# Layer-2 matrices: another order of loads and splits, with part of the split on GpSimd

## What is computed

```python
x = x + L0(x): x @ W0.T + bias0 + scale[id0] * (x @ A0[id0].T) @ B0[id0].T
x = x + L1(x): x @ W1.T + bias1 + (x @ A1[id1].T) @ B1[id1].T
x = x + L2(x): einsum('bsi,boi->bso', x, weight2[id2])      # 8 matrices of 1024 x 1024
x = x + L3(x): einsum('bct,bcd->bdt', x, weight3[id3])      # 64 x 64, over the rows
```

## Time and profile before

| what | us |
|---|---|
| median of 3 runs | 625.91 |
| the runs | 622.2, 625.91, 628.33 |
| the profiled execution's own time | 622.85 |
| its span in the trace | 621.0 |
| PE busy in the span | 587.2 |
| DVE busy | 327.2 |
| ACT busy | 278.9 |
| POOL busy | 58.6 |

### The profile page before, as it was taken

How to read it: one execution, slowest core, us unless ns; L and a number is a source line. 1 busy time by engine, 2 the same in 40 slices (tenths; PEclk the granted TensorE clock), 3 DMA queues, 4 the chain that set the end, 5 groups by cost and what they waited for, 6 DMA issues and landing times.

```text
span 621.0 us, 11131 instructions
## 1 busy us (share of the span) xinstructions
PE 587.2 (95%) x2742; PEld 485.2 (78%) x2743; DVE 327.2 (53%) x579; ACT 278.9 (45%) x369; POOL 58.6 (9%) x87
## 2 busy tenths in 40 slices
PE   8999999999998998699999869999995998999997
PEld 7888878888777886588888658888884885888885
DVE  6993220041796566555554774455667475555420
ACT  5632211042586283536346463635465545272412
POOL 3340001000031001000300200002010102000000
PEclk9999999999999999799999989999999999999999
DMA  8756723010053224513121552213143425031102
GB/s 318 227 167 70 86 83 138 18 52 17 5 202 137 75 72 168 202 37 97 40 68 36 194 166 82 74 33 100 36 169 106 167 57 165 19 93 44 35 1 68
DMA packets 66013, 60.92 MB, mean 98 GB/s; under 512 B 42050, under 2 KB 50242, under 8 KB 65988
## 3 DMA queue, kind: packets, MB, share of 16 engines
q1 hardware_dynamic: 65988, 60.63, 33.3%
HBM read 49.33 MB, written 11.27 MB: 98 GB/s over the span
## 4 chain that ended last, share of the span: by engine, by line
PE 76%; DVE 7%; issue 6%; SPq 3%; ACT 3%; DMA 2%; DVEq 1%; ACTq 1%; POOL 0%; POOLq 0%
PE y_ps L1172 22%; PE y_ps L1130 21%; PE y_ps L1082 11%; PE t_ps L1082 5%; PE t_ps L1161 5%; DVE ring L887 3%; PE y_ps L1063 2%; PE low_ps L1120 2%; SPq L225 1%; PE y_ps L1059 1%; PE low_ps L1063 1%; PE t_ps L1063 1%; DVE ops L905 1%; DMA a_stage<-a_tab 1%; PE y_ps L1188 1%
## 5 line engine op out<-in xcount | busy, mean ns | idle before, releaser
L1172 PE MATMUL y_ps<-ring,ops 128*128 128x512 f32 (+1 forms) x792 | 191.5, 395 | 5.9 <-issue 3.3
L1130 PE MATMUL y_ps<-wm,ops 128*128 128x512 f32 x768 | 180.0, 391 | 0.0
L1172 PEld LDWEIGHTS y_ps<-ring,ops 128*128 128x128 f32 (+1 forms) x792 | 146.3, 188 | 40.1 <-issue 4.8
L1130 PEld LDWEIGHTS y_ps<-wm,ops 128*128 128x128 f32 x768 | 141.9, 188 | 29.0 <-DVE arena L894 0.2
L887 DVE TENSOR_TENSOR ring<-arena,ring 128x1024 fp32r<-128x1024 f32 x40 | 48.1, 1250 | 24.3 <-ACT ring L551 19.1
L1082 PE MATMUL y_ps<-ring,wm 128*128 128x512 f32 x240 | 55.3, 390 | 0.0
L1161 PE MATMUL t_ps<-w_split,ops 128*128 128x256 f32 x256 | 38.2, 295 | 17.1 <-DVE ops L905 14.8
L1161 PEld LDWEIGHTS t_ps<-w_split,ops 128*128 128x128 f32 x256 | 36.4, 201 | 21.1 <-DVE ops L905 16.1
L524 ACT CAST ops<-arena 128x512 fp32r<-128x512 f32 x32 | 19.4, 622 | 73.3 <-PE y_ps L1130 73.3
L1082 PEld LDWEIGHTS y_ps<-ring,wm 128*128 128x128 f32 x240 | 44.9, 188 | 9.3
L432 POOL TENSOR_TENSOR arena<-arena,ident 128x128 f32<-128x128 f32 x40 | 28.0, 710 | 232.5 <-DMA arena<-wt 228.7
(11 more groups left out here) (144 smaller groups left out, 604.6 us busy)
## 6 DMA issues: line engine op xcount, KB each, us to landing
arena<-wt SPq DMA_DIRECT2D x48, 512.0 KB, 4.6
arena<-xt SPq DMA_DIRECT2D x32, 256.0 KB, 2.8
out<-arena SPq DMA_DIRECT2D x30, 256.0 KB, 3.1
arena<-w SPq DMA_DIRECT2D x8, 576.0 KB, 5.2
a_stage<-a_tab SPq DMA_DIRECT2D x64, 64.0 KB, 1.9
arena<-b_tab SPq DMA_DIRECT2D x64, 64.0 KB, 2.0
arena<-a_cols SPq DMA_DIRECT2D x8, 256.0 KB, 4.1
a_tab<-bias SPq DMA_DIRECT2D x4, 256.0 KB, 8.5
```

The costliest lines, as they stand in the source:

```text
L1130: op = nc.tensor.matmul(y_ps[:, cols], xs[:, k, part_x, :], wm[:, k, part_w, cols], start=k == 0 and part_x == part_w, stop=False)
L1172: op = nc.tensor.matmul(y[0:m, cols], xs2[:, k, part_x, 0:m], ring[:, k, part_w, cols], start=k == 0 and part_x == part_w, stop=k == KT - ...
```

## The change

Loads: SP reads x and a one pair further ahead (`x_and_a(j + 2)`), and puts both ahead of the chunks; b and w3 stay at one pair ahead. Split: GpSimd makes the lo tile of tiles 3 and 7, behind its own addition to that chunk, with a semaphore of its own (`w_lo_pool`); DVE makes the other six. Requests for chunk 7 wait for GpSimd's tile 3. ACT converts tiles 0 to 3 of the next matrix ahead of `b_again_parts`. `xs2_hi` and `xs2_lo` of the first half come ahead of the next tiles, and in a mixed pair between the two halves of its second matrix. `half_used` is now signalled by the last matmul of the last first half. Tiles 5 and 6, 7 stand around `x_hi`, and `take_x2` ahead of the second `x_lo`. At the start, tiles 0 to 4 of the first matrix are converted while the last product with W1 still runs (`w1_used`, signalled tile by tile), and the two groups of transposes of step 1 stand 12 and 10 matmuls earlier than they did: the first ahead of the second half of the product with M, the second ahead of its last tile. The table holds the rank of the second and of the next matrix (`second_of`, `next_of`) instead of flags. What is computed is the same.

```diff
+        BY_DVE = HK - 1
+
+        def halves_ready(eng, rank, h):
+            eng.wait_ge(w_lo, (2 * BY_DVE) * rank + (h + 1) * BY_DVE)
+            eng.wait_ge(w_lo_pool, 2 * rank + (h + 1))
...
             def load_chunk(matrix, rank, k):
                 if not (isinstance(rank, int) and rank == 0 and k < STAGES):
-                    sp.wait_ge(w_lo, rank * KT + (k - STAGES + 1))
+                    h, n = divmod(k, HK)
+                    if n < BY_DVE:
+                        sp.wait_ge(w_lo, (2 * BY_DVE) * rank + ((h - 1) * BY_DVE + n + 1))
+                    else:
+                        sp.wait_ge(w_lo_pool, 2 * rank + h)
...
+            def step(j):
+                b_rows(j + 1)
+                store(j - 2)
+                layer3_of(j + 1)
+                x_and_a(j + 2)
+                after_next(j - 2)
+                behind_layer2(j - 1)
+
+            x_and_a(1)
+            other_chunks(0)
+            b_rows(1)
+            layer3_of(1)
+            x_and_a(2)
+            first_chunks(1)
...
                     nc.gpsimd.tensor_tensor(diag, diag, ident[:, :], ALU.add).then_inc(w_folded, 1)
+                    if k % HK == BY_DVE:
+                        pool.wait_ge(w_hi, rank * KT + (k + 1))
+                        nc.gpsimd.tensor_tensor(ring[:, k, 1, :], w_stage[:, k % STAGES, :], ring[:, k, 0, :],
+                                                ALU.subtract).then_inc(w_lo_pool, 1)
...
+            def convert_first(tiles):
+
+                for k in tiles:
+                    if k < KT - 1:
+                        act.wait_ge(w1_used, k + 1)
+                    else:
+                        act.wait_ge(product_done, DONE_M + KT)
+                    convert(0, (k,))
...
+            def behind_layer2(j, between=None):
+
+                second, following = second_of(act, j), next_of(act, j)
+                with act.If(second != 0):
+                    convert_second(second, j, FIRST_HALF)
+                xs2_hi(j + 1, 0)
+                with act.If(second != 0):
+                    convert_second(second, j, SECOND_HALF)
                 with act.If(following != 0):
                     act.wait_ge(half_used, j + 1)
-                    convert(rank + mixed + 1, FIRST_HALF)
+                    convert(following, FIRST_HALF)
...
                 split_w3(j)
-                second_half_of_next(j - 2, SECOND_HALF[1:])
+                second_half_of(before, j - 2, SECOND_HALF[1:2])
                 if not last:
-                    for h in range(2):
-                        x_hi(j + 1, h)
+                    x_hi(j + 1, 0)
+                second_half_of(before, j - 2, SECOND_HALF[2:])
+                if not last:
+                    x_hi(j + 1, 1)
                 x2_hi(j)
                 if not last:
                     b_hi_parts(j + 1)
                 behind_layer2(j - 1)
-                xs2_hi(j, 0)
                 if not last:
                     for layer in range(2):
                         b_again_parts(layer)
-                first_half_of_next(j - 1)
...
             take_m(6)
+            convert_first(range(5))
             take_m(7)
...
             def convert(rank, tiles):
                 for k in tiles:
+                    if k % HK == BY_DVE:
+                        continue
                     dve.wait_ge(w_hi, rank * KT + (k + 1))
...
                 for k in (FIRST_HALF, SECOND_HALF)[h]:
+                    ends_half = final and k in (HK - 1, KT - 1)
...
-                            if final and k == HK and part_x == part_w and cols is BANKS[0]:
-                                op.then_inc(half_used, 1)
...
-                    if final and k == KT - 1:
-                        op.then_inc(l2_done, 1)
+                    if ends_half:
+                        op.then_inc(half_used if k == HK - 1 else l2_done, 1)
...
-                with pe.If(mixed != 0):
-                    first_part()
+                with pe.If(second != 0):
+                    first_part(False)
                     layer2_half(y, 1, tiles=True)
-                    pe.wait_ge(w_lo, rank * KT + (KT + HK))
-                    layer2_half(y, 0, ROWS)
-                    pe.wait_ge(w_lo, rank * KT + (KT + KT))
+                    halves_ready(pe, second, 0)
+                    layer2_half(y, 0, ROWS, final=True)
+                    halves_ready(pe, second, 1)
                     last_part(ROWS)
...
-                main_part(1, (lambda: transposes(0, 0)) if before == 1 else None)
+                if before == 1:
+                    transposes(0, 0)
+                main_part(1, (lambda: transposes(0, 1)) if before == 1 else None)
                 lora_b(j)
-                if before == 1:
-                    transposes(0, 1)
```

More of the change, by code:

```diff
@@ L349, in store @@
                     sp.dma_start(out[batch], out_rows[b * ROWS:(b + 1) * ROWS, :]).then_inc(stored, 16)
[L351 to L365, removed]
-                if before == 1:
[L367 to L373, removed]
-                    rank, mixed, following = first_rank(sp, j - 1), mixed_of(sp, j - 1), following_of(sp, j - 1)
-                    with sp.If(mixed != 0):
-                        other_chunks(rank + 1)
-                        first_chunks(rank + 2)
-                    with sp.If(following != 0):
-                        other_chunks(rank + mixed + 1)
@@ L381, in _, with x_and_a @@
-            step(0, before=0)
-            step(1)
-            with sp.Fori(2, PAIRS - 1) as j:
-                step(j, before=2)
-            step(PAIRS - 1, before=2, last=True)
-            rank, mixed, following = (f(sp, PAIRS - 2) for f in (first_rank, mixed_of, following_of))
-            with sp.If(following != 0):
-                first_chunks(rank + mixed + 2)
+            def x_and_a(j):
+                sp.wait_ge(x_lo_ready, 2 * j)
+                load_x(j)
+                which = loras(j)
+                sp.wait_ge(a_lo_ready, j)
+                load_a(which)
@@ L390, in _ @@
+            first_chunks(1)
+            b_rows(2)
+            layer3_of(2)
+            x_and_a(3)
+            behind_layer2(0)
+            with sp.Fori(2, PAIRS - 2) as j:
+                step(j)
+            b_rows(PAIRS - 1)
+            store(PAIRS - 4)
+            layer3_of(PAIRS - 1)
+            after_next(PAIRS - 4)
+            behind_layer2(PAIRS - 3)
+            store(PAIRS - 3)
+            after_next(PAIRS - 3)
+            behind_layer2(PAIRS - 2)
             store(PAIRS - 2)
-            rank, mixed = first_rank(sp, PAIRS - 1), mixed_of(sp, PAIRS - 1)
@@ L392, in _ @@
-            with sp.If(mixed != 0):
-                other_chunks(rank + 1)
+            after_next(PAIRS - 2)
+            second = second_of(sp, PAIRS - 1)
+            with sp.If(second != 0):
+                other_chunks(second)
             batches = of_pair(T_BATCH, BATCHES - 2, BATCHES - 1)
@@ L436, in fold_w3, with of_step @@
                 nc.gpsimd.tensor_tensor(w3_stage[:, :], w3_stage[:, :], ident[:, :], ALU.add).then_inc(w3_folded, 1)
+            def of_step(j):
+                if not (isinstance(j, int) and j < 2):
+                    before = next_of(pool, j - 2)
+                    with pool.If(before != 0):
+                        fold(before, SECOND_HALF)
+                second, following = second_of(pool, j - 1), next_of(pool, j - 1)
+                with pool.If(second != 0):
+                    fold(second, range(KT))
+                with pool.If(following != 0):
+                    fold(following, FIRST_HALF)
             fold_w3(0)
@@ L972, in step @@
                 split_w3(j)
-                second_half_of_next(j - 2, SECOND_HALF[1:])
+                second_half_of(before, SECOND_HALF[1:2])
                 if not last:
-                    for h in range(2):
-                        x_lo(j + 1, h)
+                    x_lo(j + 1, 0)
+                second_half_of(before, SECOND_HALF[2:])
                 take_x2(j)
+                if not last:
+                    x_lo(j + 1, 1)
                 x2_lo(j)
@@ L1017, in _ @@
             xs2_lo(j - 1, 1)
-            second_half_of_next(j - 2, SECOND_HALF)
-            behind_layer2(j - 1)
+            second_half_of(next_of(dve, j - 2), SECOND_HALF)
+            second = second_of(dve, j - 1)
+            with dve.If(second != 0):
+                convert(second, range(KT))
         @block.tensor
```

203 lines of the change are left out of this document (109 added, 94 removed).

## The result

The changed kernel takes 600.44 us (median; 599.55 to 600.83) against 625.54 of the kernel before in the same comparison: a ratio of 0.960, 95% interval 0.955 to 0.965. The forecast was 600.5. The profiled execution took 599.55, 1.75 more than its span.

A forecast was written before the change was run, and what follows sets the result against it. PE, busy for 95% of the span, was taken as the bound, with 37.9 us lost in disturbed places. Terms 28.1 + 3.5 - 7.7 = 23.9 took span 621.0 to 597.1; execution and median allowances gave 600.5 us, 8-in-10 range 592 to 611.

The forecast's parts named there:

- A change of matrix: At three changes of matrix (T: start of the old matrix's last layer 2): PE's waiting mostly goes, 28.1 us gained.
- P: Time of one GpSimd subtraction making a lo tile of 1024 columns: 2.8 us, bounds 1.2 to 5.7.
- the port decides: Rival: GpSimd and DVE hold each other up at changes and the mixed pair; +12 us, 612.5 us; chance 0.12.
- The mixed pair: Pair using two matrices (T1: its start): the new order makes its last half late; 7.7 us lost.
- SP's count of reads and issues: Before the mixed pair's chunk request: 28 table reads (19.3 us), 28 issues (14), seven branches (1.4); request at T1+13.
- The lower bound, chunks in time: Mixed pair's smallest loss: chunks there in time, subtraction 1.2 us, no fall of the clock; 3.4 us lost.
- The start: Kernel start: the 2.25 us wait for `xs2_lo`, 0.8 of issue and some refill go; 3.5 us gained.
- SP's queue full: Rival in SP's loads: b or w3 rows become late instead of a; half of 28 us lost, 614.5; chance 0.05.
- slower through P: Rival at GpSimd's subtraction: no gain at P = 5.6, 635 us at P = 7; chance 0.03.
- from 3 us on: At a change of matrix: PE waits of 3 us or more also cost 1.7 us through the lower clock.
- Sum: Whole kernel: gains at the changes and start less the mixed pair's loss, 23.9 us off the span, to 597.1.

## Why the prediction was right

- **A change of matrix.** Right in size, and in the cause of the larger part. Forecast 28.1, measured 28.2: against twice 25.7, 0.52, 0.50 and 0.65 are left a change instead of 0.6. The cause named, x2 late and the clock behind it, makes 4.9 and 1.7 of the 9.8 to 10.3 lost a change. The sum took the rest as gained too, without a term for it. Most of it was PE's waits for LoRA parts and "issue", 2.1 to 2.3 a change; that they went as well was not argued, and in that the sum was lucky. Both orders undone give back 22.4 of the 28.2; the 5.8 left stay with the rest of the change, among it x's splits and the table, which the forecast did not price. The a rows were asked for at T+7.1, the first chunk at T+12.45 (forecast 12.7), the fourth was out by T+15.3 (15.7). One step of it was off and did little harm: POOL's tile 7 came at T+23.2, not T+24.9, and held `x_lo` instead of tile 6, for 2.2; x2 ends at T+31.4, between the T+29.4 without POOL and the T+32.5 with it. PE wants it at T+31.1.
- **GpSimd's price.** P = 2.8, and the mean of ten is 2.805, but that they agree is luck. The 2.8 was scaled from an undisturbed addition and stands for an undisturbed subtraction. The two that met no DVE instruction took 2.39 (the first) and 2.34 (the last). The other eight started beside DVE and took 2.54 to 3.11, since their time in the trace holds the wait: the 3.11 shown ends 2.25 behind DVE's row, the 2.91 ends 2.26 behind DVE's tile 6. The estimate of 2.2 plus dispatch that the prediction worked out from the Trainium skill ("GPSIMD Engine Reference", section 3.1) was nearer to the undisturbed time.
- **The port.** The rival "the port decides" had the mechanism right (the 2.88 for 0.68 above) and its price wrong. The Trainium skill's rule in "SBUF — State Buffer", section "SBUF: two separate sides", is borne out at its full strength, a whole instruction held for another whole one. At a change the new order leaves room for it, and GpSimd's part cost 2.9 us in all, not 12 more than forecast. In the kernel before, with both `x_lo` ahead of the taking of x2, it cost 13.6. What the forecast did not see is that GpSimd's part is a loss by itself: it was priced on the path, never against leaving it out.
- **The mixed pair.** Forecast 7.7 lost, measured 8.3. The request came at T1+14.4 instead of T1+13, the last subtraction at T1+24.6 took 2.34 instead of 2.8, and the restart came at T1+27.0 instead of T1+26.1; the fallen clock cost 1.4 in 18 matmuls, 1.7 forecast. The mis-sized term is SP's count of reads and issues. The lower bound, chunks in time, assumed that nothing else was late at T1+25.1; the runs give T1+26.3 for that.
- **The start.** 3.7 for 3.5, and the waits of 2.25 and 0.83 are gone as forecast. What the runs add is that these 3.7 hold against the kernel before; against the nearly old start with GpSimd's part it is 6.1.
- **SP's queue full; slower through P.** Neither showed: PE waits for no DMA at a change, and P stayed at half of 5.6. The "from 3 us on" for the clock was a guess between the 2.60 that left it up and the 4.92 that did not; a wait of 3.12 also left it up.
- **Sum.** 28.1 + 3.5 - 7.7 = 23.9 forecast, 28.2 + 3.7 - 8.3 = 23.6 measured, span down by 23.2. The 600.5 held to 0.1 also because the median lies only 0.9 above the profiled execution, where 1.5 had been put on.

## What to carry to other kernels

When a helper engine shares a port, price its work against leaving it out, and look at which instruction of the other engine it will stand beside: ten subtractions moved off DVE cost 3 us in the new order, 14 in the kernel before, where they fell on operations that the critical path waits for, and nothing that could be measured where one of those operations had been moved out of their way. When two orders feed one wait, undo both before you judge either: at the changes of matrix they cost 16 us taken back apart and 22 together, and in the mixed pair each alone moved the restart by 0.7 where both moved it by 4.3. A gain of 28 can hide a loss of 8 in a stretch with another limit, so compare stretch by stretch even when the total comes out as forecast, and give every part of a stretch's loss a term before you count it as gained.

## What the runs showed of the hardware

- A short DVE operation with two inputs in SBUF that starts beside GpSimd's subtraction ends only after it: 0.68 became 2.88 (0.54 behind the end of the subtraction), two that take 0.76 became 2.97, and two of 1.55 became 3.64. It holds the other way too: a subtraction that takes 2.34 to 2.39 alone took 3.11 beside DVE's row of three. The taking of x2, which reads PSUM, kept its 1.23 beside a subtraction.
- In the mixed pair TensorE's granted clock fell to the lower of its two levels after every wait of 4.7 to 9.0 us: 18 matmuls then took 5.6 to 7.1, with no order by the length of the wait (9.00 gave 5.75, 7.21 gave 7.07). After 2.60, 2.90 and 3.12 it stayed (4.35 to 4.37). Two waits close together, 2.96 and 0.97, brought it down (24 matmuls in 7.22), and 2.25 and 0.83 did not (5.75). At the third change of the run with GpSimd's part alone it fell after 1.45, 0.68 and 0.95 (24 matmuls in 7.35); at the second, 1.31, 0.50 and 0.93 left it up (5.72). With ACT's casts undone PE waited 1.0 and 1.8 at each of the three changes; the clock stayed at the first two (18 matmuls in 4.27) and fell at the third (5.89), so the waits alone don't decide it.
